# A graph layer on one core: deeper gather rings, single buffers with new stage orders, and a throttled head

## The reference

```python
h = x @ W_in2f
Wij = (ssp(rbf @ Wf1 + bf1) @ Wf2 + bf2) * dist_cut      # ssp = softplus - log 2
x_ij = h[idx_j] * Wij                                    # idx_j = dst
m = segment_sum(x_ij, idx_i, num_segments=n_atoms)       # idx_i = src
m = ssp(m @ Wo1 + bo1) @ Wo2 + bo2
out = layernorm(x + (x + m))
```

## Time and profile before

| | us |
|---|---|
| three runs | 1859.76, 1863.84, 1867.15 |
| median | 1863.84 |
| profiled execution | 1858.28 |
| its span | 1856.5 |
| busy PE, DVE, ACT, POOL | 1697.3, 1489.3, 1492.9, 1441.4 |
| DMA moved | 363.47 MB |
| mean granted TensorE clock | 0.972 of full |

### The profile page before, as it was taken

The page is one execution under the profiler, slowest core; times in us unless marked ns, Lnnn a source line. Parts: engine busy times, 40 slices in busy tenths (PEclk is TensorE's granted clock), DMA queues, the critical chain, the costliest instruction groups (busy, mean ns, idle before and its releaser), DMA issues. The chain is left out here.

```text
span 1856.5 us, 36676 instructions
## 1 busy us (share of the span) xinstructions
PE 1697.3 (91%) x11376; PEld 1532.2 (83%) x11376; DVE 1489.3 (80%) x3750; ACT 1492.9 (80%) x2945; POOL 1441.4 (78%) x1385
## 2 busy tenths in 40 slices
PE   3499899999999999999999998889976999999995
PEld 2378788888888888888888887778866999999995
DVE  2477788787888888888888786777765999999996
ACT  2477788778888788888888786776756999999996
POOL 7422488888887888878888888888754999999997
PEclk9699999999999999999999998999998999999998
DMA  9799866656566665666665666665675999999994
GB/s 354 251 356 372 266 123 112 126 112 125 115 125 122 112 123 114 124 125 112 125 120 116 119 122 113 114 118 108 116 185 170 333 363 362 360 360 364 357 366 174
DMA packets 177341, 363.47 MB, mean 196 GB/s; under 512 B 25622, under 2 KB 76264, under 8 KB 177148
## 3 DMA queue, kind: packets, MB, share of 16 engines
q1 hardware_dynamic: 101128, 257.75, 39.8%
q0 software_dynamic: 75136, 102.45, 32.4%
q10 hardware_dynamic: 884, 0.92, 0.2%
HBM read 206.90 MB, written 154.12 MB: 194 GB/s over the span
## 5 line engine op out<-in xcount | busy, mean ns | idle before, releaser
L354 POOL DMA_INDIRECT acc<-sums,src_ix x392 | 637.2, 1626 | 141.6 <-issue 116.0
L341 POOL DMA_INDIRECT xg<-in_x,dst_t x392 | 401.4, 1024 | 215.6 <-issue 114.6
L780 DVE SCALAR_TENSOR_TENSOR m_l<-pair,wgt_t,m_h 128x256 fp32r<-128x256 f32 x392 | 171.6, 479 | 230.5 <-ACT m_h L621 206.6
L385 POOL TENSOR_SCALAR sums<-sums,neg_mean,rstd 128x256 f32<-128x256 f32 x392 | 283.2, 733 | 10.2
L495 PE MATMUL pair<-m_h,same 128*128 128x256 f32 (+1 forms) x980 | 244.8, 285 | 30.4 <-ACT sums L628 21.9
L621 ACT ACTIVATE m_h<-pair,wgt_t 128x256 fp32r<-128x256 f32 x392 | 165.0, 475 | 99.5 <-PE pair L409 57.6
L495 PE MATMUL pair<-m_l,same 128*128 128x256 f32 (+1 forms) x980 | 241.8, 281 | 0.0
L409 PE MATMUL pair<-wo_h,msg_h 128*128 128x256 f32 (+1 forms) x784 | 230.9, 295 | 6.0 <-DVE m_l L780 5.2
L495 PEld LDWEIGHTS pair<-m_h,same 128*128 128x128 f32 (+1 forms) x980 | 185.1, 189 | 52.2 <-issue 34.9
L576 ACT ACTIVATE zs<-pair,bf 128x512 f32<-128x512 f32 x196 | 124.1, 685 | 125.8 <-PE pair L433 99.5
L409 PE MATMUL pair<-wo_h,msg_l 128*128 128x256 f32 (+1 forms) x784 | 222.0, 283 | 0.0
(11 more groups left out here) (97 smaller groups left out, 5249.8 us busy)
## 6 DMA issues: line engine op xcount, KB each, us to landing
acc<-fill SPq DMA_DIRECT2D x197, 256.0 KB
xg<-in_x SPq DMA_DIRECT2D x97, 512.0 KB, 6.4
sums<-acc SPq DMA_DIRECT2D x97, 512.0 KB, 6.8
out<-sums SPq DMA_DIRECT2D x97, 512.0 KB, 4.7
attr<-in_edge_attr SPq DMA_DIRECT2D x196, 128.0 KB
srcb<-in_src_rows SPq DMA_DIRECT2D x98, 256.0 KB
xg<-in_x,dst_t POOLq DMA_INDIRECT x392
acc<-sums,src_ix POOLq DMA_INDIRECT x392
```

The lines of the kernel that those rows point to most:

```text
L341: pool.indirect_dma_start(xg[0:g.p, g.xs, r], None, t["x"], bass.IndirectOffsetOnAxis(ap=dst_t[0:g.p, r, g.n:g.n + 1], axis=0)).then_inc(x ...
L354: pool.indirect_dma_start(acc, bass.IndirectOffsetOnAxis(ap=src_ix[g.slot][0:g.p, r:r + 1], axis=0), sums[0:g.p, g.slot, r], None, compute ...
L385: last = pool.tensor_scalar(normed[0:g.p, g.n % NRING, r], res[0:g.p, u, r], neg_mean[0:g.p, u, r:r + 1], rstd[0:g.p, u, r:r + 1], ALU.add ...
L780: dve.scalar_tensor_tensor(out=m_l[0:g.p, r], in0=bank[6][0:g.p, k * D:(k + 1) * D], scalar=col(wgt_t, r, g), in1=m_h[0:g.p, r].bitcast(F3 ...
```

## The change

It does five things.

1. Rings and lead: RING 12 to 14, XRING 11 to 17, AHEAD 23 to 30.
2. In the head, the gather of group g < 30 also waits until (g-8)//2+1 groups have been turned.
3. Clears: 198 through one function, at most four in flight, each waiting for the landing of the one four before; the pause after 8 clears goes.
4. SBUF is saved for the rings: `x_h`, `x_l`, `ssp_h`, `ssp_l` and `same` have one copy, not two; `ssp` and `msg` are gone, their values are written over the matmul's result in PSUM (banks 2, 3 and 5) and the high and low parts read them there. So `filter1` waits for `ssp_low` of the group before, `w_of` for `msg_low`, and x_high, x_low, ssp_high, ssp_low, compare for the last reader of the group before. Small tensors are laid over others, and the order of allocation changes. In the second phase `ssp2` lies in `sums`, its parts in `ssp_h`/`x_h` and `ssp_l`/`x_l`.
5. New orders and lags of the stages of PE, ACT and DVE; `compare` is cut into its four parts; the biases are made ahead of step 0. Sixteen of the 17 first reads of x for the second phase move from behind SP's edge loop into its last iterations.

```diff
-RING = 12
-XRING = 11
+RING = 14
+XRING = 17
-AHEAD = 23
-EARLY_CLEARS = 8
+AHEAD = 30
+FREE = 8
+IN_FLIGHT = 4
...
-        x_h, x_l = (sb(n, [P, 2, H, R, P], F32R) for n in ("x_h", "x_l"))
+        x_h, x_l = (sb(n, [P, H, R, P], F32R) for n in ("x_h", "x_l"))
-        zs, ssp = (sb(n, [P, H, 512]) for n in ("zs", "ssp"))
-        ssp_h, ssp_l = (sb(n, [P, 2, H, R, P], F32R) for n in ("ssp_h", "ssp_l"))
+        zs, h_sb = (sb(n, [P, H, 512]) for n in ("zs", "h_sb"))
+        ssp_h, ssp_l = (sb(n, [P, H, R, P], F32R) for n in ("ssp_h", "ssp_l"))
...
+                    a, b = c * CLEAR * P, min((c + 1) * CLEAR * P, N + R * P)
+                    wait(sp, cleared[c % IN_FLIGHT], c // IN_FLIGHT * 16)
...
-            clear_to(EARLY_CLEARS)
-            sp.wait_ge(xg_in[0], 16 * R)
             clear_to(FIRST_CLEARS)
...
                 clear_to(FIRST_CLEARS + (n - 1) * CLEARS_A_STEP)
+                if G - XRING <= n - 2:
+                    fetch_x(group((n - 2) % XRING))
...
-                        wait(pool, xt_ps, (g.n - XRING + 1) * 2)
+                        turned = max(g.n - XRING + 1, (g.n - FREE) // 2 + 1 if g.n < AHEAD else 0)
+                        wait(pool, xt_ps, turned * 2)
...
-                wait(pe, ssp_sb, g.n * H)
+                wait(pe, sspl_sb, g.n * H)
...
-                    wait(pe, msg_sb, g.n * H + m)
+                    wait(pe, msgl_sb, g.n * H + m)
...
-            run((w_of(1), 2), (summed(0), 3), (h_of(0), 1), (summed(1), 3), (filter1, 0), (turn_x(0), 0),
-                (out1(0), 2), (turn_x(1), 0), (w_of(0), 1), (h_of(1), 1), (out1(1), 2), before={1: filter_bias})
+            run((w_of(1), 2), (summed(1), 3), (turn_x(0), 0), (turn_x(1), 0), (out1(0), 2), (h_of(0), 1), (filter1, 0),
+                (w_of(0), 1), (out1(1), 2), (h_of(1), 1), (summed(0), 2), before={1: filter_bias})
...
-                    wait(act, h_ps, (g.n - 1) * H)
+                    wait(act, h_ps, g.n * H)
...
-                    high(ssp_h[:, g.par, h], ssp[:, h].rearrange("m (r e) -> m r e", r=R), ssph_sb)
+                    wait(act, w_ps, g.n * H)
+                    high(ssp_h[:, h], bank[2 + h][:].rearrange("m (r e) -> m r e", r=R), ssph_sb)
...
-            run((keep_y(0), 4), (msg_high(1), 3), (ssp_high(0), 2), (ssp_high(1), 2), (keep_h(0), 2), (absolute(0), 1),
-                (absolute(1), 1), (expo(0), 1), (m_high(0), 3), (keep_y(1), 4), (expo(1), 1), (x_high(0), 1), (loga(0), 1),
-                (loga(1), 1), (x_high(1), 1), (keep_h(1), 2), (m_high(1), 3), (a_high, 0), (msg_high(0), 2), before={1: weights})
+            run((x_high(0), 1), (keep_y(0), 3), (x_high(1), 1), (ssp_high(0), 1), (msg_high(1), 2), (ssp_high(1), 1), (keep_y(1), 3),
+                (a_high, 0), (m_high(0), 2), (keep_h(0), 1), (absolute(0), 0), (absolute(1), 0), (expo(0), 0), (expo(1), 0),
+                (loga(0), 0), (loga(1), 0), (msg_high(0), 1), (m_high(1), 2), (keep_h(1), 1), before={1: weights})
...
-                    wait(dve, msgl_sb, (g.n - 1) * H + m + 1)
-                    dve.scalar_tensor_tensor(out=msg[:, m], in0=bank[5][:], scalar=bias_w[:, m:m + 1], in1=h_sb[:, m],
+                    dve.scalar_tensor_tensor(out=bank[5][:], in0=bank[5][:], scalar=bias_w[:, m:m + 1], in1=h_sb[:, m],
...
-                    dve.scalar_tensor_tensor(out=ssp[:, h], in0=bank[2 + h][:], scalar=neg_bf1[:, h:h + 1], in1=zs[:, h],
+                    dve.scalar_tensor_tensor(out=bank[2 + h][:], in0=bank[2 + h][:], scalar=neg_bf1[:, h:h + 1], in1=zs[:, h],
...
-            run((m_low(0), 3), (message(0), 2), (x_low(0), 1), (softplus(0), 1), (softplus(1), 1), (x_low(1), 1),
-                (m_low(1), 3), (message(1), 2), (a_low, 0), (msg_low(0), 2), (target, 3), (msg_low(1), 2), (ssp_low(0), 1),
-                (ssp_low(1), 1), (compare, 2), before={1: first_weights, 2: tables, 3: second_weights})
+            run((x_low(0), 1), (message(1), 2), (x_low(1), 1), (msg_low(1), 2), (ssp_low(0), 1), (ssp_low(1), 1), (a_low, 0),
+                (compare(0), 2), (m_low(0), 2), (compare(1), 2), (compare(2), 2), (message(0), 1), (compare(3), 2), (softplus(0), 0),
+                (msg_low(0), 1), (softplus(1), 0), (m_low(1), 2), (target, 2),
+                before={0: biases, 1: first_weights, 2: tables, 3: second_weights})
```

More of the change, by code:

```diff
@@ L449, in stage @@
                     transposed(m, bank[4][:].rearrange("f (r e) -> f r e", r=R)[:, :, 0:g.p], w_in_h, w_in_l,
-                               [x_h[:, g.par, k, :, 0:g.p] for k in range(H)], [x_l[:, g.par, k, :, 0:g.p] for k in range(H)]).then_inc(h_ps, 1)
+                               [x_h[:, k, :, 0:g.p] for k in range(H)], [x_l[:, k, :, 0:g.p] for k in range(H)]).then_inc(h_ps, 1)
                 return stage
@@ L494, in stage @@
                             for m in (m_h, m_l):
-                                last = pe.matmul(o, same[0:g.p, g.par, FROM[a] + b - a, 0:g.p], m[0:g.p, a],
+                                last = pe.matmul(o, same[0:g.p, FROM[a] + b - a, 0:g.p], m[0:g.p, a],
                                                  start=a == 0 and m is m_h, stop=a == b and m is m_l)
@@ L526, in stage @@
                             for sp2, w in ((ssp2_h, wo2_h), (ssp2_h, wo2_l), (ssp2_l, wo2_h)):
-                                last = pe.matmul(o, sp2[:, g.par, h, r, 0:g.p], w[:, h, :], start=False, stop=h == H - 1 and sp2 is ssp2_l)
+                                last = pe.matmul(o, sp2[g.par][:, h, r, 0:g.p], w[:, h, :], start=False, stop=h == H - 1 and sp2 is ssp2_l)
                     last.then_inc(o_ps, 1)
@@ L727, in stage @@
                     dve.wait_ge(xh_sb, g.n * 2 + q + 1)
-                    wait(dve, h_ps, (g.n - 1) * H)
-                    low(x_l[:, g.par, :, 2 * q:2 * q + 2, 0:g.p], bank[q][:].rearrange("f (h k e) -> f h k e", h=H, k=2)[:, :, :, 0:g.p],
-                        x_h[:, g.par, :, 2 * q:2 * q + 2, 0:g.p], xl_sb)
+                    wait(dve, h_ps, g.n * H)
+                    low(x_l[:, :, 2 * q:2 * q + 2, 0:g.p], bank[q][:].rearrange("f (h k e) -> f h k e", h=H, k=2)[:, :, :, 0:g.p],
+                        x_h[:, :, 2 * q:2 * q + 2, 0:g.p], xl_sb)
                 return stage
```

123 lines of the change are left out of this document (62 added, 61 removed).

## The result

The changed kernel takes **1890.78 us** (median of 4, 1882.41 to 1891.13) beside 1862.67 (4, 1859.76 to 1867.15): a ratio of 1.0138, 95% interval 1.0103 to 1.0173. It is 1.4% slower; the forecast was 1834 us, with a range of 1802 to 1876. The profiled execution took 1891.1 us with a span of 1889.3.

What follows compares the result with a forecast made beforehand. GpSimd's list was taken to bound the edge phase, then TensorE's ring of waits: 207 + 85 x 13.3 + 31.5 ends it at 1369 us, 29 earlier; 1858.3 less 29 is 1829, plus 5.6 to the median, 1834 us; range 1802 to 1876.

Steps and rivals of the forecast that it cites:

- 13th turn: Head: the 13th group is turned at 207 us, bounds 195 and 228, where it was 222.4.
- last clear: Head: last of 198 clears at 198 us: 45 for the first 36, 140 for 162 at 0.865, 13 for extra gathers.
- 13th to last turn: Middle of the edge phase: 85 steps of 13.3 us, 1130.5 us, putting the last turn at 1337.5 us.
- second phase, added: After the edge phase: ScalarE sets the pace at 4.37 us a group, so 0 us, between 0 and -8.7.
- The head: Start of the edge phase: throttled gathers and four clears in flight bring the 13th group's turn to 207 us.
- the hole of 60 to 80 us: Head: stretch moving only 195 GB/s, VectorE waiting 37.64 us without visible releaser; supposed to close because queues are shallow.
- The step of 13.3 us: Edge phase: time per group set by a chain of waits across ScalarE, VectorE and TensorE, bounds 12.9 and 13.8 us.
- The unknown price of writing into PSUM: VectorE's writes in each step: perhaps 8 ns quicker or 0.1 us dearer each; taken as nothing.
- The tail: Last turn to end of scatters: 31.5 us, from 5, thinning steps 10 and 8, sums 2, scatters and wait 6.
- the third: Rival, head: throttle does not close the hole, 13th turn at 228 us, 1855 us, no change; chance 0.16.
- rival 2: Edge phase, msg_low(1) to out1(0): longer step; at 13.9 us the kernel takes 1885 us, slower; chance 0.22.
- the ring: Edge phase: cycle of waits from filter1 through ScalarE, VectorE and TensorE, closing at 13.3 us, taken as the bound.

Runs made afterwards that it cites:

- after: The changed kernel with all five parts of the change, against the kernel before; 1890.78 us on record, ratio 1.0138.
- e15: The changed kernel run again unchanged, later and on another chip; 1858.36 us, 0.9973 against the kernel before.
- e18: The kernel before run again unchanged, later and on another chip; 1865.7 us, ratio 0.9996.
- e2: The changed kernel with clears not limited to four in flight, throttle on gathers kept; 1883.28 us, 1.0079 against the kernel before.
- e6: The changed kernel with VectorE's target moved from the end of its step to behind compare(3); 1887.96 us, 1.0124 against the kernel before.
- e14: Changed kernel; groups 2 to 12: every second waits until earlier gathers landed; later bursts split, target behind compare(3), 27 groups ahead; 1867.73 us, 1.0023.
- e11: Changed kernel; gathers of groups 2 to 12 wait for landing of the group two before; target behind compare(3), 25 groups ahead; 1891.53 us, 1.014.
- e13: Changed kernel; every second group of gathers ahead waits until all gathers before it have landed; 1861.11 us, 0.9973 against the kernel before.
- e1: The changed kernel without the two-for-one rule on gathers in the head; 1903.13 us, 1.0193 against the kernel before.
- e9: The kernel before; gathers of groups 2 to 10 wait for the landing of the group two before; 1867.47 us, 1.0000.
- e5: The changed kernel; each group of gathers ahead waits until the former group has landed; 1894.94 us, 1.0143 against the kernel before.
- e4: The kernel before, gathers of groups 11 to 22 sent in bursts of eight every second step; 1877.92 us, 1.0066.
- e8: The kernel before; each group of gathers ahead waits until the former group has landed; 1874.78 us, 1.0046.
- e12: The kernel before; every second group of gathers ahead waits until all gathers before it have landed; 1867.41 us, 1.0000.
- e17: The kernel before with every second group of gathers ahead waiting for all earlier landings, run again on another chip; 1866.26 us, 1.001.
- e16: The changed kernel with every second group of gathers ahead waiting for all earlier landings, run again on another chip; 1857.99 us, 0.9975.

## Why the prediction was wrong

The forecast of the span was 1856.5 - 29 = 1827.5 us. Its terms against both sorts of chip:

```
us                           forecast   after (record)   after on the other sort (e15)
13th turn                    207        253              221
last clear                   198        255.0            222.8
13th to last turn            1130.5     1139             1133.5
last turn to end of scatters 31.5       39.1             39.1
second phase, added          0          0                +1
span                         1827.5     1889.3           1852.8
```

**The head is the step that failed.** "This supposes that the hole of 60 to 80 us closes because the queues are shallow." It does not close: the hole is TensorE's updates, which come late on the chip of the record as long as GpSimd's gathers keep coming, and the throttle does not bound the first burst, for two turns come early (16 and 27 us) and let twelve groups go, until 65 us. Worse, the rule that was to spare the queues sends gathers in bursts of eight, with updates 4 to 5 us late in every step of the head. I had the trace of that in hand: the 37.64 us of the earlier trace rows "with no visible releaser". I read it as a full queue of clears; it was the only row that spoke of another mechanism, and no term of the sum was worked out for its staying and growing. Together that is 253 - 221 = 32 us, by the same program on the other sort of chip; there the hole closes in the kernel before as well (102 matmuls from 60 to 80 us in e18, 33 in the earlier trace rows), so the shallow queues are not what closes it.

**The second fault in the head is a mis-sized term**, on the other sort of chip as well: 0.865 us a clear and 368 GB/s were taken over from a kernel without the cap. In e15 the 162 clears after the first 36 take from 48 to 223 us, 1.08 us each, while 335 GB/s move; the last clear is 25 us later than forecast, the 13th turn 14. The cap has a part in this, how large is open. On the cap the Trainium skill, "DMA: Bandwidth & Descriptors", section "Queues, rings and completion order", was the better guide: by its turn-taking of queue rows a cap wins nothing, and e2, without it, was not slower than after (0.4% under its median, with overlapping intervals).

**The step of 13.3 us was right**, and for the reason given. On the record it is 13.39 us in the middle and 8 us too much over the 85 steps; where no update is late it is 13.20 (e15: 3637 matmuls in 600 us). The chain runs through abs, exp, ln, msg_high, VectorE and msg_low to out1, and moving target out of VectorE's part shortens it by 0.35 us (e6) and by 0.29 (e14 against e15). In e11 that gain does not show (13.5 us); there updates are later than in e6, 0.35 us in the mean. The unknown price of writing into PSUM, in groups by form, after, 280 to 1280 us:

```profile
L769 DVE SCALAR_TENSOR_TENSOR pair<-pair,bias_w,h_sb 128x512 f32<-128x512 f32 x149 | 112.4, 754 | 64.6 <-PE pair L413 54.2 <-issue 7.1 <-remote 3.3
...
L676 DVE TENSOR_TENSOR msg_l<-pair,msg_h 128x512 fp32r<-128x512 f32 x150 | 103.7, 692 | 31.3 <-ACT msg_h L559 21.6 <-issue 4.1
```

Message into PSUM takes 754 ns (745 into SBUF before), msg_low from PSUM 692 (687 from SBUF). Taking nothing for it was right. The 62 cycles that the Trainium skill, "VectorE: DVE Perf Modes", section "The TRN2 errata", puts on a PSUM read are not there.

**The tail was 7.6 us too short.** The last turn to the end of the last scatter takes 39.1 us in both runs. ScalarE's first sums of the last three groups, then GpSimd's first scatters of the last four, after:

```profile
1401.79 0.64 ACT L632 ACTIVATE sums<-pair 128x512 f32<-128x512 f32 x1
...
1412.38 0.62 ACT L632 ACTIVATE sums<-pair 128x512 f32<-128x512 f32 x1
...
1421.50 0.59 ACT L632 ACTIVATE sums<-pair 84x512 f32<-84x512 f32 x1
```

```profile
1390.52 1.63 POOL L358 DMA_INDIRECT acc<-sums,src_ix  x1 [4.06 <-DVE src_ix L762]
...
1403.20 1.55 POOL L358 DMA_INDIRECT acc<-sums,src_ix  x1 [5.06 <-DVE src_ix L762]
...
1413.76 1.55 POOL L358 DMA_INDIRECT acc<-sums,src_ix  x1 [2.95 <-DVE src_ix L762]
...
1424.24 1.48 POOL L358 DMA_INDIRECT acc<-sums,src_ix  x1 [3.08 <-DMA acc<-sums,src_ix]
```

From the last turn at 1392.2 the rest of the step takes 9.6 us and not 5, the two thinning steps 10.6 and 9.1 and not 10 and 8; and behind the last sums at 1422.1 come the wait for the landing of the former group and four scatters, 9.2 us, where I counted two scatters and the wait as 6 (my terms add up to 31, not 31.5). GpSimd's waits name target (src_ix), which had become the last stage of VectorE's step, but it is not what I missed: in e6, where target comes early, the tail is 38.5 us.

**The rest.** GpSimd does not starve TensorE (right); the second phase stays at its pace (right). Of the rivals, the third, "the head gains nothing", 13th turn at 228 and 1855 us, is close to what the kernel does where updates are on time (221, 1858), and it had named the clears' waits for landings. The measured time lies above the range of 1802 to 1876 us, and on the chip of the record none of the rivals came out: rival 2 put the slower outcome into the ring, at 13.9 us a step, and the ring was as forecast. A fast and a slow side were foreseen, the place of the slow one was not.

## What to carry to other kernels

A long wait with no visible releaser is a row to explain before anything is built on its going away: work out the sum with it staying and with it growing. A rate measured in one regime (a full queue of clears) is not the rate of the regime that a cap makes of it. And where a gain or a loss is some per cent and hangs on such a wait, measure the same program on more than one chip, and the first one again at the end, before crediting an edit: e13 looked like a cure of 30 us, and the unedited kernel gained as much by the change of place.

## What the runs showed of the hardware

- **TensorE's semaphore updates can arrive late while GpSimd's indirect DMAs keep coming**: 5 us behind a burst of eight gathers, 2 behind one of four, up to 41 to 46 behind an unbroken run (after, e1, e9); those of VectorE and ScalarE that are on record never by more than 0.01 us in the edge phase. When the gathers run dry before every group, at about half the pace, at most 0.9 us until 80 us and 2.6 until 200 (e5); a limit of eight under way, which held hardly anything back, changed nothing (e9).
- **It depends on the chip, or on something that changed with it.** The two records and the chips of e1 to e4, e5 to e8 and e9 to e11 show it; those of e12 to e14, e15 to e17 and e18, all used later, do not, at all. The traces that show it also miss records of updates and landings, the others hardly any, so a part of the profiler in it is not ruled out. The kernel before takes the same time on both sorts (1865.1, 1865.3, 1866.9 beside 1866.1, 1865.5, 1866.2 us), since GpSimd's list takes back what its head gains; after takes 1891 and 1858 us. What differs, and why TensorE alone is touched, stays open. Whether a drain before every second group helps on a chip with late updates also stays open: e12 to e14 and e16, e17 never ran on one.
- **Four clears of 256 KB in flight move less than an open number**: 371 GB/s at a DMA share of 1.00 against 408 at 1.05, from 20 to 40 us in after and e2.
